# A mixture-of-experts and linear-attention kernel: the first expert tile is loaded one stage earlier, and the matrix of the last closed sequence is made inside the expert loop

## The reference: what is computed

```python
# attention branch, 32 heads of 16 channels, relu instead of softmax
q, k, v = relu(xn @ qkv_weight.T)                    # v gets a column of ones
vk   = einsum('bnhe,bnhd->bhed', v_pad, k)           # summed over the whole sequence
vk_q = einsum('bhed,bnhd->bnhe', vk, q)
y    = (vk_q[..., :D] / (vk_q[..., D:] + EPS)) @ proj_weight.T + proj_bias

# expert branch, 8 experts, the best 2 of each token
cont = sigmoid(xn @ enc_w + enc_b) @ s2c_w + s2c_b   # 64 numbers for a token
eh   = relu(cont @ e_w1 + e_b1); eo = eh @ e_w2 + e_b2
out  = layernorm(sigmoid(sigmoid((eo * comb) @ c2s_w + c2s_b) @ dec_w + dec_b)) * ln_g + ln_b
```

## Time and profile before

| what | value |
|---|---|
| median of three runs | 1964.83 us |
| the profiled execution's own time | 1968.65 us |
| its span (first to last instruction) | 1966.8 us |
| TensorE busy | 1891.9 us, 96% of the span |
| VectorE, ScalarE, GpSimd busy | 1137.2, 750.0, 377.4 us |
| mean granted TensorE clock | 0.987 of full speed |

### The profile page before, as it was taken

How to read it: one execution, slowest core, us unless ns; L and a number is a source line. 1 busy time by engine, 2 the same in 40 slices (tenths; PEclk the granted TensorE clock), 3 DMA queues, 4 the chain that set the end, 5 groups by cost and what they waited for, 6 DMA issues and landing times. The chain is left out here.

```text
span 1966.8 us, 24863 instructions
## 1 busy us (share of the span) xinstructions
PE 1891.9 (96%) x8988; PEld 1565.0 (80%) x8988; DVE 1137.2 (58%) x2043; ACT 750.0 (38%) x1265; POOL 377.4 (19%) x417
## 2 busy tenths in 40 slices
PE   7999999999999999998999989999999999999997
PEld 5888888887788888886788768888888888888885
DVE  6555555553442222223788656777777777777776
ACT  4454555544211222112677523333333333333333
POOL 1000000000004444420000122222222222222220
PEclk9999999999999999998999999999999999999998
DMA  5561332442123332222877511222222222222211
GB/s 207 224 241 67 143 148 100 170 154 77 65 87 117 115 114 80 113 104 98 299 230 236 190 52 70 91 91 91 92 90 91 84 80 83 87 90 82 91 48 65
DMA packets 74826, 233.95 MB, mean 119 GB/s; under 512 B 9856, under 2 KB 15952, under 8 KB 68176
## 3 DMA queue, kind: packets, MB, share of 16 engines
q1 hardware_dynamic: 66432, 219.58, 31.0%
q0 software_dynamic: 8272, 12.76, 2.0%
HBM read 151.95 MB, written 80.36 MB: 118 GB/s over the span
## 5 line engine op out<-in xcount | busy, mean ns | idle before, releaser
L106 PE MATMUL A_E<-xs,enc_h 128*128 128x512 f32 x512 | 207.4, 405 | 0.0
L1317 POOL DMA_INDIRECT ga<-eo_scratch,idx x64 | 65.6, 1025 | 717.4 <-DVE ratel L1560 536.7
L108 PE MATMUL A_E<-xs,enc_h 128*128 128x512 f32 x512 | 200.8, 392 | 0.0
L107 PE MATMUL A_E<-xs,enc_l 128*128 128x512 f32 x512 | 200.5, 392 | 0.0
L1470 PE MATMUL D_D<-dec_h,rateh 128*128 128x512 f32 x512 | 200.0, 391 | 0.0
L1471 PE MATMUL D_D<-dec_l,rateh 128*128 128x512 f32 x512 | 199.7, 390 | 0.0
L1472 PE MATMUL D_D<-dec_h,ratel 128*128 128x512 f32 x512 | 199.4, 389 | 0.0
L566 DVE TENSOR_TENSOR spl<-sp_t,sph 128x512 fp32r<-128x512 f32 x128 | 88.6, 692 | 191.5 <-ACT sph L388 189.8
L861 POOL DMA_INDIRECT slots_scratch<-ctok,idx x128 | 123.4, 964 | 243.1 <-DVE v L994 120.7
L384 ACT ACTIVATE sp_t<-A_E,cols 128x512 f32<-128x512 f32 x128 | 88.2, 689 | 195.0 <-PE A_E L108 193.9
L994 DVE SCALAR_TENSOR_TENSOR v<-B_KV,v 128x512 fp32r<-128x512 f32 x64 | 44.3, 692 | 172.5 <-ACT v L890 172.5
(11 more groups left out here) (263 smaller groups left out, 4785.7 us busy)
## 6 DMA issues: line engine op xcount, KB each, us to landing
xs_scratch<-xs SPq DMA_DIRECT2D x16, 2048.0 KB, 8.6
xsd<-xs_scratch SPq DMA_DIRECT2D x16, 2048.0 KB, 7.9
xs<-xs_scratch SPq DMA_DIRECT2D x14, 2048.0 KB, 8.8
wt<-ew_scratch SPq DMA_DIRECT2D x39, 513.0 KB, 3.7
x<-in_x SPq DMA_DIRECT2D x16, 1024.0 KB, 5.4
xd<-in_x SPq DMA_DIRECT2D x16, 1024.0 KB, 5.4
out_y<-out SPq DMA_DIRECT2D x64, 256.0 KB, 2.0
slots_scratch<-zt SPq DMA_DIRECT2D x1, 9984.0 KB
```

The source lines that it names most:

```text
L106: pe.matmul(out, w_hi, x_hi, start=start, stop=False)
L107: pe.matmul(out, w_lo, x_hi, start=False, stop=False)
L108: return pe.matmul(out, w_hi, x_lo, start=False, stop=stop)
L1317: pool.indirect_dma_start((gb if second else ga)[:, i % 2, t, :], None, d["eo"][:, :], bass.IndirectOffsetOnAxis(ap=T["idx2" if second els ...
```

## The change

A load of tile 0's slots and weights (`load_slots`, `load_expert`, now functions of their own) is issued by SyncE at the end of `keyvalue`, after the last load of x and after all scatters have landed; its buffers and `cl` get places in the on-chip memory that `keyvalue` leaves free. The ones in `cl` are written by VectorE at the start of `keyvalue`, from `ones`; the memset on GpSimd is dropped. In tile 63 `project(63, "v")` stands ahead of `outer(62)`. In `experts`, `turn_in(0)` and step 0 come first, and the second matrix is made in pieces behind the steps 2 (`turn`), 4 to 7 (`project`, one each, into the banks `bO[1]`, `bY`, `bT`, `bY`) and 8 (`spread`).

```diff
+    put("BCc", "wt0", [P, EW], F32R)
+    put("BCc", "gt0", [P, NT, P])
+    put("BCc", "cl", [P, 2, BLK], F32R)
...
@@ keyvalue, SyncE
+            for t in range(4):
+                sp.wait_ge(S[f"slot_in{t}"], 16 * 2 * TT // 4)
+            sp.wait_ge(S["eidx_out"], 1)
+            load_slots(sp, d, T, S, 0)
+            load_expert(sp, d, T, S, 0)
+            sp.wait_ge(S["gt_in0"], 16)
+            sp.wait_ge(S["wt_in0"], 32)
@@ keyvalue, TensorE
                 project(n, "k")
+                if n == TT - 1:
+                    project(n, "v")
                 if n:
                     outer(n - 1)
...
-                project(n, "v")
+                if n < TT - 1:
+                    project(n, "v")
             outer(TT - 1)
@@ keyvalue, VectorE, ahead of tile 0
+            for i in range(2):
+                dve.tensor_copy(T["cl"][MOE:P, i, :], f32(T["ones"][MOE:P, 0:1]).broadcast_to([MOE, BLK]))\
+                    .then_inc(S["cl_ones"], 1)
@@ experts
+        M_AT, KS_AT, m_bank = (4, 5, 6, 7), 8, (bO[1], bY, bT, bY)
@@ experts, SyncE
-            load_slots(0)
-            for g in range(NS):
-                load_expert(g)
+            next_slots(1)
+            for g in range(1, NS):
+                next_expert(g)
@@ experts, GpSimd
-            pool.memset(T["eo"][0:MOE, 0, :], 1.0).then_inc(S["c_consts"], 1)
@@ experts, ScalarE
-            turn_act(act, T, S, 1, bY)
-            for g in range(KC):
-                project_act(act, T, S, 0, 1, g, bH[g])
-            spread_act(act, T, S, 0, 1, bO[0])
+            def matrix(n):
+                if n == 2:
+                    turn_act(act, T, S, 1, bY)
+                if n in M_AT:
+                    g = M_AT.index(n)
+                    project_act(act, T, S, 0, 1, g, m_bank[g])
+                if n == KS_AT:
+                    spread_act(act, T, S, 0, 1, bY)
@@ experts, ScalarE, in the loop behind hidh
+                matrix(n)
@@ experts, TensorE
-            turn_pe(pe, T, S, 1, bY)
-            for g in range(KC):
-                project_pe(pe, T, S, 1, g, bH[g])
-            spread_pe(pe, T, S, 1, bO[0])
+            def matrix(n):
+                if n == 2:
+                    turn_pe(pe, T, S, 1, bY)
+                if n in M_AT:
+                    g = M_AT.index(n)
+                    if g == 2:
+                        pe.wait_ge(S["cl_out"], 3)
+                    elif g == 3:
+                        pe.wait_ge(S["ml_out"], KC + 2)
+                    project_pe(pe, T, S, 1, g, m_bank[g])
+                if n == KS_AT:
+                    pe.wait_ge(S["ml_out"], BATCH * KC)
+                    spread_pe(pe, T, S, 1, bY)
@@ experts, TensorE, turn_in
+                if g == 3:
+                    pe.wait_ge(S["ml_out"], KC + 3)
@@ experts, TensorE, turn_out
                 if g == 0:
-                    pe.wait_ge(S["vtl_out"], 2)
+                    pe.wait_ge(S["ks_out"], BATCH)
@@ experts, TensorE, first
                 if n >= 4:
                     pe.wait_ge(S["hidl_out"], n - 3)
-                else:
-                    pe.wait_ge(S["ml_out"], KC + n + 1)
@@ experts, TensorE, second
-                    if g == 0:
-                        pe.wait_ge(S["ks_out"], BATCH)
+                    if g == 1:
+                        pe.wait_ge(S["ml_out"], KC + 1)
@@ experts, VectorE
-            close_products(dve, T, S, 1)
-            turn_dve(dve, T, S, 1, bY)
-            dve.wait_ge(S["c_consts"], 1)
-            for i in range(2):
-                dve.tensor_copy(cl[MOE:P, i, :], T["eo"][0:MOE, 0, :]).then_inc(S["cl_ones"], 1)
...
-            for g in range(KC):
-                project_dve(dve, T, S, 0, 1, g, bH[g])
             content(0)
+            close_products(dve, T, S, 1)
```

More of the change, by code:

```diff
@@ L205, in place @@
     put("B", "lates", [P, NS])
-    for i in range(4):
-        put("Cc", f"wt{i}", [P, EW], F32R)
+    put("BCc", "wt0", [P, EW], F32R)
+    put("BCc", "gt0", [P, NT, P])
+    put("BCc", "cl", [P, 2, BLK], F32R)
     for i in range(3):
+        put("Cc", f"wt{i + 1}", [P, EW], F32R)
+        put("Cc", f"yo{i}", [P, NT, MOE])
+    for i in range(1, 3):
         put("Cc", f"gt{i}", [P, NT, P])
-        put("Cc", f"yo{i}", [P, NT, MOE])
     put("Cc", "ch", [P, 2, BLK], F32R)
-    put("Cc", "cl", [P, 2, BLK], F32R)
     put("Cc", "hidh", [P, 4, BLK], F32R)
@@ L825, in dispatch_dve, with load_slots, load_expert @@
         yield
+def load_slots(sp, d, T, S, g):
+    sp.dma_start(T[f"gt{g % 3}"][:, :, :], d["slots"][g * BLK:(g + 1) * BLK, :].rearrange("(p j) c -> p j c", j=NT))\
+        .then_inc(S[f"gt_in{g % 3}"], 16)
+def load_expert(sp, d, T, S, g):
+    e = sp.value_load(T["eidx"][0:1, g:g + 1], min_val=0, max_val=NE - 1)
+    rows, wt = P if g < 4 else BIAS_ROWS, T[f"wt{g % 4}"]
+    sp.dma_start(f32(wt[:, 0:B2 + 2]), d["ew"][bass.ds(e, 1), :, 0:B2 + 2].rearrange("e p w -> (e p) w"))\
+        .then_inc(S[f"wt_in{g % 4}"], 16)
+    sp.dma_start(f32(wt[0:rows, E1B:EW]), d["ew"][bass.ds(e, 1), 0:rows, E1B:EW].rearrange("e p w -> (e p) w"))\
+        .then_inc(S[f"wt_in{g % 4}"], 16)
 def keyvalue(nc, d, T, S):
@@ L1046, in _, with next_slots, next_expert @@
         def _(sp):
-            def load_slots(g):
+            def next_slots(g):
                 if g >= 3:
                     sp.wait_ge(S["tin_done"], g - 2)
-                sp.dma_start(gt[g % 3][:, :, :], d["slots"][g * BLK:(g + 1) * BLK, :]
-                             .rearrange("(p j) c -> p j c", j=NT)).then_inc(S[f"gt_in{g % 3}"], 16)
-            def load_expert(g):
+                load_slots(sp, d, T, S, g)
+            def next_expert(g):
                 if g >= 4:
@@ L1056, in load_expert @@
                     sp.wait_ge(S["eo_out"], g - 3)
[L1057 to L1063, removed]
+                load_expert(sp, d, T, S, g)
             def store(g):
@@ L1068, in store @@
                     .then_inc(S[f"eo_stored{g % 3}"], 16)
-            load_slots(0)
-            for g in range(NS):
-                load_expert(g)
+            next_slots(1)
+            for g in range(1, NS):
+                next_expert(g)
                 if g + 1 < NS:
-                    load_slots(g + 1)
+                    next_slots(g + 1)
                 if g == 2:
@@ L1206, in _, with matrix @@
         def _(dve):
-            close_products(dve, T, S, 1)
-            turn_dve(dve, T, S, 1, bY)
-            dve.wait_ge(S["c_consts"], 1)
-            for i in range(2):
-                dve.tensor_copy(cl[MOE:P, i, :], T["eo"][0:MOE, 0, :]).then_inc(S["cl_ones"], 1)
+            def matrix(n):
+                if n == 2:
+                    turn_dve(dve, T, S, 1, bY)
+                if n in M_AT:
+                    g = M_AT.index(n)
+                    project_dve(dve, T, S, 0, 1, g, m_bank[g])
             def content(g):
```

## The result

The kernel after takes 1960.69 us (median of 8 runs, 1957.02 to 1962.9), the kernel before 1964.51 us beside it (8 runs, 1963.33 to 1967.4). The ratio is 0.9974, interval 0.9965 to 0.9984: some 0.26%, or 3.8 us at these medians, where 4.3 were predicted.

The account below looks back on a forecast made before the run. TensorE, busy 96%, was taken as the bound. 917.04 + 4.54 + 19.6 + 1.8 + 2.45 put `first(16)` at 945.4 instead of 949.77, 4.3 us gained: median 1964.83 to 1960.5, 8-in-10 range 1957.5 to 1964.8.

Parts of the forecast that it names:

- v first: End of the key and value stage: v of tile 63 ahead of `outer(62)` starts the next stage 0.96 us earlier.
- Tile 0's load hidden: Expert stage start: tile 0 has landed 26 us ahead, so `first(0)` starts 2.13 us into the stage.
- `turn_in(1)` at T + 4.54: T is the expert stage's start; TensorE idles 1.7 us for tile 1's slots, landing taken as 4.5 us.
- the page's case: Expert stage start: tile 1's slots land in 2.6 us, TensorE hardly waits, result 1959.2 us.
- Two new waits, 1.8 us: TensorE waits 0.7 to 0.8 us at `spread` for `ml` and 1.0 at `turn_out(0)` for `ks`.
- Low clock, 2.45 us: Start of the expert stage: 4.9 us at 1.2 GHz after work resumes, costing half of itself.
- Loads, 0: Tiles 3 and 4: the 0.95 us of waits are gone or nearly, 0 to 0.8 us, with 2 us margin.
- Rival 1: Tile 3's weights and tile 4's slots land 2 to 4 us later than forecast; 1961.5 to 1963 us; chance 0.15.
- The long wait unchanged: After `first(16)`: VectorE's wait for a store of `yo` stays, with 3 to 4 us on TensorE.
- rival 3: Clock is kept at the stage's start or at the long wait; 1957.8 us; chance 0.07.
- Rival 2: Clock falls again at the waits for `ml` and `ks`, or stays low to 930; 1962.9 us; chance 0.11.
- Rival 4: Tile 1's slots land late at the stage's start; 1968.9 us at 12.9 us landing; chance 0.07 with anything else slower.

Follow-up runs that it names:

- the pair without the long wait: e9 and e7: the kernels before and after, each with the xsd load cut into eight pieces; 1958.91 and 1954.56 us.
- e1: Kernel before with only v of tile 63 projected ahead of `outer(62)`; 1963.65 us, ratio 0.9992.
- e7: Kernel after with the 2 MB load of xsd cut into eight, one per tile; 1954.56 us, ratio 0.9942.
- e12: Kernel after with the spreading of `ks` moved behind `turn_in(0)`, into bank `bO[1]`; 1961.20 us, ratio 0.9979.
- e5: Kernel after with the spreading of `ks` moved from step 8 to step 4; 1960.09 us, ratio 0.9973.
- e6: Kernel after with five unused matmuls behind `outer(63)` and five behind `turn_in(0)`; 1961.46 us, ratio 0.9975.
- e10: e6 with the four big loads issued one tile later, behind tile 3's weights and tile 4's slots; 1959.95 us, ratio 0.9970.
- e3: Kernel after without the early fetch of tile 0 and with v of tile 63 in its old place; 1964.62 us, ratio 0.9996.
- e2: Kernel before with only tile 0's slots and weights loaded in the key and value stage; 1964.86 us, ratio 1.0000.
- e9: Kernel before with the 2 MB load of xsd cut into eight, one per tile; 1958.91 us, ratio 0.9965.
- e8: Kernel after with the edits of e5, e6 and e7 together; 1954.46 us, ratio 0.9942.
- e4: Kernel after, unchanged, run once more to see its scatter; 1961.83 us, ratio 0.9979.

## Why the prediction was right, and where it was lucky

The forecast was 1960.5, the result 1960.69, and the pair without the long wait gives 4.35 us where the sum had 4.3. In the main the mechanism is the predicted one: the first tile starts at once, the matrix is made inside the loop with its twelve matmuls at full clock, and two new waits take part of the gain. But four of the signs that I had named failed: the stage starts at 916.25 and not near 917.04 (by time won ahead of tile 63's k), `turn_in(1)` waits for no DMA at all, the clock is back at 922.8 and not from 925.4 on, and `first(16)` is at 942.57 and not within 1 us of 945.4. Step by step:

- **v first, 0.96 us.** Right: the stage ends 0.97 us sooner after the last matmul of k in the trace, and 0.98 in e1, which has this edit alone.
- **Tile 0's load hidden.** Right: `turn_in(0)` waits only for the change of stage (1.56 us, as e7 and e12 do too), and `first(0)` starts 2.57 us after SyncE's first issue; 2.13 was predicted (the terms given for it add up to 2.07), and e5, e6 and e10, where the clock was up, have 2.12 and 2.13. The rest is the low clock, which already covers `turn_in(0)`.
- **`turn_in(1)` at T + 4.54, after 1.7 us of idle for a DMA.** Wrong: there is no such wait. It starts at T + 3.56 because the queue ahead of it ran at the low clock; in e6, at full clock, it starts at 2.74. The row of 4.5 us did not carry over; 256 KB of slots as the stage's first load landed in 2.5 to 2.7 us in all nine profiles with the order of after, and in e1 and e3, in 3.6 in e2, and in 4.6 only in e9. Even my lower bound, 3.8, was too high. The Trainium skill (DMA: Bandwidth & Descriptors, Anatomy of one DMA), from which 2.6 us was worked out, lies closer to the trace of after than the row did, though its sentence is on GpSimd's transfers; it does not explain the 4.5. (The 1959.2 that I gave for the page's case doesn't follow from my terms: 1.9 us less than 1960.5 is 1958.6.)
- **Two new waits, 1.8 us.** Right. The idle in brackets, 0.50 and 0.83 us, is less than what they cost, since it counts from the end of a matmul that shows 0.39 us while the next could start after 0.23. From start to start, as the sum had it, they are 932.39 - 931.73 = 0.66 and 935.24 - 934.23 = 1.01, together 1.67 us.
- **Low clock, 2.45 us.** The fall came as said; the clock was back 3.0 us after `turn_in(1)`, not 4.9. From there to the mark after needs 22.76 us; less 19.6 of work and 1.67 of waits, 1.49 are left, half of the 3.0 us. So the working was right and the length wrong, by 0.96 us. That is not what the low clock costs the kernel: e6 prices the whole slow stretch at 1.24 us up to `first(8)`, because at full clock part of the work waits for VectorE (0.64 us in e6).
- **Loads, 0.** Right in the result, since TensorE waits for none, but with a margin of 0.5 us and not 2. In e5, e6, e8 and e12 tile 3's weights land 21.0 to 21.3 us into the stage whatever TensorE does, and after asks at 21.74. Rival 1 was the next thing to bind, and does as soon as anything else is mended.
- **The long wait unchanged.** Right as a wait (3.36 us against 3.47). Its clock was not a constant: what rival 3 called the clock kept happened in this profile (12.88 us from `first(32)` to `first(40)`), in e5, and not in e4, e6 or e12. So it scatters from profile to profile, and belongs in the range, not in a rival of the change. Rival 2, a second fall at the two new waits, didn't happen: the clock is 1.00 from 923 to 943.

Summed from the stage's start, I predicted 28.39 us to `first(16)` and it is 26.32: 0.98 from the landing, 0.13 from the waits, 0.96 from the clock. But I set this against a before of 31.77, in which the clock was slow to return and the loads of the tiles 3 and 4 were late; with the 30.03 of e1 and e9 the change gains 0.97 + 3.71 = 4.7 us. Two errors, of 2.1 and 1.7 us, cancelled. The direction and most steps hold, but that the number agrees so well is luck.

Rival 4 (a late landing) is refuted: no first load of the stage took above 4.6 us in fourteen profiles. Not settled is why the landing is 4.5 us in before and e9 and 2.7 in e1, which differs from before only by the order of v, and what decides the clock's outcome at the start and at the long wait.

## What to carry to other kernels

An early fetch doesn't bring a tile forward while other work stands ahead of it, and moving that work away only uncovers the wait for the load: plan the two together, and ask of each what is late next. A small load or store that is issued right behind a large one can land late; looking at what is issued just ahead of the transfer that an engine waits for gave more here (6 us for one load cut in eight) than moving the work. And before a sum is set against one profile of the kernel before, see in a second profile whether its clock came back as it usually does: in that stretch two traces of the same order of work differed by 1.7 us here.

## What the runs showed of the hardware

- **The same code, the same resumption, two clocks.** With work resumed at 922.11 and 922.12, TensorE's clock returned to 2.4 GHz at 927.3 in the one profile and at 925.0 in the other. It had fallen at 917.1 in the one and at 918.2 in the other, in the same gap, so the stretch at 1.2 GHz was 10.2 and 6.8 us long. The Trainium skill (TensorE: Matmul & The Clock Gate, Part 1) says that the number of slow matmuls at a start varies between runs, and the traces agree: 1.06 us at `first(0)`.
- **Unused matmuls hold the clock.** With five behind the last `outer` and five behind `turn_in(0)`, it was 1.00 throughout the start of the stage (e6); without, 0.50 for 6.8 us. That was worth 1.24 us, and only with the loads reordered did it reach the end (e6 0.3 us, e10 1.4 us on the mark).
- **A small store behind a large load.** 128 KB behind 2 MB landed after 10.0 us, and with the load cut in pieces after 6.1, and VectorE's wait for it fell from 4.07 to 0.2 us.
- **Landings behind a full queue.** 256 KB took 13.1 us behind four big loads of 3.8 MB, against 2.5 us for the same size as the first load of the stage (4.5 in before).
